# A small product turned round: router logits by expert instead of by token, and the way back to token order

## The reference, cut to what matters

```python
router_probs = jax.nn.softmax(jnp.einsum('bsh,he->bse', x, w_router), axis=-1)
gate_weights = jax.nn.softmax(jnp.einsum('bsh,he->bse', x, w_gating) / GATE_TEMP, axis=-1)
g = jnp.einsum('bsh,ehf->ebsf', x, w_gate)
u = jnp.einsum('bsh,ehf->ebsf', x, w_up)
h = jax.nn.silu(g) * u
expert_out = jnp.einsum('ebsf,efh->ebsh', h, w_down)
cw = router_probs * gate_weights
cw = cw / (jnp.sum(cw, axis=-1, keepdims=True) + 1e-09)
out = jnp.einsum('ebsh,bse->bsh', expert_out, cw)
```

## Time and profile before

| | |
|---|---|
| median of 3 runs | 1175.09 us (1173.66 to 1175.84) |
| the profiled execution | 1174.75 us |
| its span | 1172.9 us |
| granted TensorE clock over the span | 0.992 |
| TensorE busy | 1143.5 us (97%) |
| VectorE busy | 928.8 us (79%) |
| ScalarE busy | 677.4 us (58%) |
| GpSimd busy | 636.2 us (54%) |

### The profile page before, as it was taken

How to read it: one execution, slowest core, us unless ns; L and a number is a source line. 1 busy time by engine, 2 the same in 40 slices (tenths; PEclk the granted TensorE clock), 3 DMA queues, 4 the chain that set the end, 5 groups by cost and what they waited for, 6 DMA issues and landing times.

```text
span 1172.9 us, 16867 instructions
## 1 busy us (share of the span) xinstructions
PE 1143.5 (97%) x5190; PEld 943.3 (80%) x5190; DVE 928.8 (79%) x2032; ACT 677.4 (58%) x1293; POOL 636.2 (54%) x496
## 2 busy tenths in 40 slices
PE   5899999999999999999999999999999999999996
PEld 4678888888888888888888888888888888888885
DVE  8788787787878878787887878778787887878665
ACT  3366565656556566565656656565655656556553
POOL 4467464555546455564655546455554645556453
PEclk8999999999999999999999999999999999999999
DMA  4230110101111020110101111010111102011110
GB/s 122 64 111 25 46 45 34 40 20 46 46 43 49 1 72 19 45 46 37 41 15 57 35 46 46 32 42 19 46 46 41 50 1 72 19 46 37 37 46 10
DMA packets 43097, 49.75 MB, mean 42 GB/s; under 512 B 3424, under 2 KB 24576, under 8 KB 43008
## 3 DMA queue, kind: packets, MB, share of 16 engines
q1 hardware_dynamic: 43008, 48.67, 13.4%
HBM read 44.20 MB, written 4.46 MB: 41 GB/s over the span
## 4 chain that ended last, share of the span: by engine, by line
PE 95%; DVE 3%; issue 1%; POOL 0%; ACT 0%; DMA 0%; POOLq 0%; SPq 0%; ACTq 0%; DVEq 0%
PE g L240 10%; PE u L240 10%; PE u L242 10%; PE u L241 10%; PE g L242 10%; PE g L241 10%; PE y L242 10%; PE y L240 10%; PE y L241 10%; PE n_ps L247 2%; PE m_ps L240 1%; PE m_ps L242 1%; PE m_ps L241 1%; PE y L263 1%; PE m_ps L321 1%
## 5 line engine op out<-in xcount | busy, mean ns | idle before, releaser
L982 POOL TENSOR_TENSOR hid_lo<-hid,hid_hi 128x512 fp32r<-128x512 f32 x255 | 342.2, 1342 | 394.5 <-ACT hid_hi L483 394.3
L477 ACT ACTIVATE gate<-g 128x512 f32<-128x512 f32 x512 | 306.3, 598 | 363.0 <-PE g L242 360.5
L723 DVE TENSOR_TENSOR hid<-gate,u 128x512 f32<-128x512 f32 x512 | 349.2, 682 | 176.9 <-ACT gate L477 121.6
L483 ACT ACTIVATE hid_hi<-hid 128x512 fp32r<-128x512 f32 x512 | 320.6, 626 | 29.4 <-DVE hid L723 28.7
L240 PE MATMUL g<-xe_hi,w_hi 128*128 128x512 f32 x512 | 207.8, 406 | 0.0
L729 DVE TENSOR_TENSOR hid_lo<-hid,hid_hi 128x512 fp32r<-128x512 f32 x257 | 205.7, 800 | 0.4
L240 PE MATMUL u<-xe_hi,w_hi 128*128 128x512 f32 x512 | 200.0, 391 | 2.3 <-DVE hid L723 2.3
L240 PE MATMUL y<-hid_hi,w_hi 128*128 128x512 f32 x512 | 199.8, 390 | 0.2 <-ACT hid_hi L483 0.2
L242 PE MATMUL y<-hid_hi,w_lo 128*128 128x512 f32 x512 | 199.8, 390 | 0.0
L242 PE MATMUL g<-xe_hi,w_lo 128*128 128x512 f32 x512 | 199.6, 390 | 0.0
L241 PE MATMUL g<-xe_lo,w_hi 128*128 128x512 f32 x512 | 199.6, 390 | 0.0
(11 more groups left out here) (155 smaller groups left out, 1146.6 us busy)
## 6 DMA issues: line engine op xcount, KB each, us to landing
cw_b<-cw_scratch SPq DMA_DIRECT2D x128, 256.0 KB, 3.6
x_sb<-x_in SPq DMA_DIRECT2D x16, 256.0 KB, 4.0
x_out<-o_sb SPq DMA_DIRECT2D x16, 256.0 KB, 2.3
stage<-wgate_in SPq DMA_DIRECT2D x8, 256.0 KB, 2.7
stage<-wup_in SPq DMA_DIRECT2D x8, 256.0 KB, 3.0
stage<-wdown_in SPq DMA_DIRECT2D x8, 256.0 KB, 3.6
cw_scratch<-cw_t SPq DMA_DIRECT2D x16, 16.0 KB, 1.4
proj<-proj_in SPq DMA_DIRECT2D x1, 136.0 KB, 2.5
```

The source lines that it names most:

```text
L477: nc.scalar.activation(gate[:, k % 2, :], g_ps[k % 2][:], ACT.Silu).then_inc(gate_ready, 1)
L483: nc.scalar.activation(hid_hi[:, k % RING, :], hid[:, k % RING, :], ACT.Copy).then_inc(hi_ready, 1)
L723: nc.vector.tensor_tensor(hid[:, k % RING, :], gate[:, k % 2, :], u_ps[k % 2][:], ALU.mult).then_inc(hid_ready, 1)
L982: nc.gpsimd.tensor_tensor(hid_lo[:, k % RING, :], hid[:, k % RING, :], hid_hi[:, k % RING, :].bitcast(f32), ALU.subtract).then_inc(lo_pool, 1)
```

## The change

- **Products.** The router's high and low parts become the weights (128 x 32 columns) and all 512 tokens the moving operand: two products into 32 partitions of `m_ps`. `router` gets a third part of zeros (through 16 more columns of `proj_in`), so that the first product is low and high against `xe_hi` and the second high and zero against `xe_lo`.
- **The way back.** VectorE transposes 32 x 32 blocks from `m_ps` to `logits_t` (after unit 27; in chunk 0 after unit 0). SyncE then issues four transfers of 16 KB within SBUF, each of 32 partitions with four pieces of 128 bytes, to `raw`, with tokens on 128 partitions. The reduce of the softmax reads `raw`.
- **Places.** The softmax moves from k = 27 to 29 on VectorE, `silus` from 28 to 29 on ScalarE; in chunk 0 the softmax, `silus`, `exps`, `products` and `weights` move one unit back. In SyncE's stream the four transfers stand after the eighth spread and before the load of the next x.
- **Warming.** 24 products of three forms come before the first `bu` (`keep_warm_split`); `keep_warm_mixed` becomes `keep_warm(18)`, and VectorE's fill of its tile goes.

```diff
-SCALAR_AT = {..., "hi_xe": 26, "silus": 28}
+SCALAR_AT = {..., "hi_xe": 26, "silus": 29}
-VECTOR_AT = {..., "lo_xe": 26, "softmax": 27, "exps": 30, "products": 31}
+VECTOR_AT = {..., "lo_xe": 26, "logits_t": 27, "softmax": 29, "exps": 30, "products": 31}
...
+            def spread_logits(c):
+                sp.wait_ge(logits_turned, c + 1)
+                if c > 0:
+                    sp.wait_ge(raw_read, c)
+                blocks = logits_t[:].rearrange("c (j b q) -> c j b q", j=NT, q=SMALL)
+                for b in range(P // SMALL):
+                    sp.dma_start(raw[b * SMALL:(b + 1) * SMALL].rearrange("p j h q -> p j (h q)"),
+                                 blocks[:, :, b, :]).then_inc(raw_loaded, 16)
...
+                if first:
+                    spread_logits(0)
                 store_cw(c, par)
...
+                if not last:
+                    spread_logits(c + 1)
...
+            def keep_warm_split():
+                w, x = proj_hi[:, 0:P], act_hi[:]
+                for cols in (SMALL, NS):
+                    for i in range(8):
+                        nc.tensor.matmul(y_ps[1][0:cols, :], w[:, 0:cols], x, start=True, stop=True)
+                for i in range(8):
+                    nc.tensor.matmul(y_ps[1][:].rearrange("p (j t) -> p j t", j=NT), w,
+                                     act_hi[:].rearrange("p (j t) -> p j t", j=NT), start=True, stop=True)
...
-                    pe.wait_ge(raw_read, c)
+                    pe.wait_ge(logits_turned, c)
...
-                for j in range(NT):
-                    t, at = slice(j * P, (j + 1) * P), 4 * E * j
-                    nc.tensor.matmul(m_ps[:, at:at + 4 * E], xe_hi[:, par, t], router[:], start=True, stop=False)
-                    last = nc.tensor.matmul(m_ps[:, at:at + 2 * E], xe_lo[:, par, t], router[:, 0, :], start=False, stop=True)
-                last.then_inc(logits_ready, 1)
+                nc.tensor.matmul(m_ps[0:4 * E, :], router[:, 0:2, :], xe_hi[:, par, :], start=True, stop=False)
+                nc.tensor.matmul(m_ps[0:4 * E, :], router[:, 1:3, :], xe_lo[:, par, :], start=False,
+                                 stop=True).then_inc(logits_ready, 1)
...
             keep_warm(WARM[1])
+            pe.wait_ge(act_hi_ready, 1)
+            keep_warm_split()
             pe.wait_ge(proj_split, 2)
...
-            keep_warm_mixed()
+            keep_warm(WARM[3])
...
+            def mix_logits_t(c):
+                dve.wait_ge(logits_ready, c + 1)
+                nc.vector.transpose(logits_t[:], m_ps[0:SMALL, :]).then_inc(logits_turned, 1)
+
             def mix_softmax_in(c):
-                dve.wait_ge(logits_ready, c + 1)
+                dve.wait_ge(raw_loaded, RAW_LOADED * (c + 1))
...
                     if first and k == 0:
+                        mix_logits_t(0)
+                    if first and k == 1:
                         mix_softmax_in(0)
-                    if first and k == 1:
+                    if first and k == 2:
                         mix_exps(0)
                         mix_products(0)
-                    if k == (2 if first else VECTOR_AT["weights"]):
+                    if k == (3 if first else VECTOR_AT["weights"]):
                         mix_weights(c)
```

More of the change, by code:

```diff
@@ L46 @@
 SCALAR_AT = {"cw_t": 3, "hi_x": 8, "du": 8, "hi_w": 13, "fin_a": 14, "fin_b": 15, "z_a": 18, "z_b": 18,
-             "hi_xe": 26, "silus": 28}
+             "hi_xe": 26, "silus": 29}
 VECTOR_AT = {"weights": 1, "stats_x": 1, "var_x": 2, "norm_x": 3, "lo_x": 7, "enter": 8, "scan": 9,
              "fin_stats": 10, "fin_var": 10, "fin_shift": 11, "leave": 12, "lo_w": 13, "y": 15, "stats_y": 16, "var_y": 16,
-             "shift": 18, "stats_x1": 22, "var_x1": 22, "norm_x1": 24, "lo_xe": 26, "softmax": 27, "exps": 30,
+             "shift": 18, "stats_x1": 22, "var_x1": 22, "norm_x1": 24, "lo_xe": 26, "logits_t": 27, "softmax": 29, "exps": 30,
              "products": 31}
@@ L58 @@
 SMALL = 32
-PROJ = P + D + 2 * E
+PROJ = P + D + 4 * E
+RAW_LOADED = 16 * (P // SMALL)
 POOL_LO = (1, 3)
@@ L121, in build @@
         proj_hi, proj_lo = sb("proj_hi", [P, P + D], f32r), sb("proj_lo", [P, P + D], f32r)
-        router = sb("router", [P, 2, 2 * E], f32r)
+        router = sb("router", [P, 3, 2 * E], f32r)
+        logits_t, raw = sb("logits_t", [SMALL, SEQ]), sb("raw", [P, NT, 2, 2 * E])
         a_col, sines = sb("a_col", [NS // 2, 1]), sb("sines", [NS // 2, P])
@@ L146, in build @@
         w_hi_done, w_lo_done = sem("w_hi_done"), sem("w_lo_done")
-        const_ready, flat_ready = sem("const_ready"), sem("flat_ready")
+        const_ready = sem("const_ready")
         proj_split, omega_ready, trig_link, trig_ready = sem("proj_split"), sem("omega_ready"), sem("trig_link"), sem("trig_ready")
@@ L157, in build @@
         xe_turned, xe_hi_ready, xe_lo_ready = sem("xe_turned"), sem("xe_hi_ready"), sem("xe_lo_ready")
-        logits_ready, raw_read, lg_ready, silus_ready = sem("logits_ready"), sem("raw_read"), sem("lg_ready"), sem("silus_ready")
+        logits_ready, logits_turned, raw_loaded = sem("logits_ready"), sem("logits_turned"), sem("raw_loaded")
+        raw_read, lg_ready, silus_ready = sem("raw_read"), sem("lg_ready"), sem("silus_ready")
         cw_ready, cw_turned, cw_t_ready = sem("cw_ready"), sem("cw_turned"), sem("cw_t_ready")
@@ L488, in _ @@
             act.wait_ge(small_loaded, 32)
-            nc.scalar.activation(router[:, 0, :], proj[:, P + D:], ACT.Copy)
+            nc.scalar.activation(router[:, 1:3, :].rearrange("p h q -> p (h q)"), proj[:, P + D:], ACT.Copy)
             nc.scalar.activation(proj_hi[:], proj[:, 0:P + D], ACT.Copy).then_inc(proj_split, 1)
@@ L658, in mix_softmax_in @@
                 pair = "p j r -> p (j r)"
-                dve.wait_ge(logits_ready, c + 1)
+                dve.wait_ge(raw_loaded, RAW_LOADED * (c + 1))
                 nc.vector.tensor_reduce(out=lg[:].rearrange("p j r e -> p j (r e)"),
-                                        in_=m_ps[:, 0:NT * 4 * E].rearrange("p (j h q) -> p j q h", j=NT, h=2),
+                                        in_=raw[:].rearrange("p j h q -> p j q h"),
                                         op=ALU.add, axis=AX.X).then_inc(raw_read, 1)
@@ L756, in _ @@
             nc.vector.memset(cw_pad[:], 0.0).then_inc(const_ready, 1)
-            nc.vector.memset(hid[:, 0, :], 0.5).then_inc(flat_ready, 1)
-            dve.wait_ge(flat_ready, 1)
-            nc.vector.tensor_copy(hid_hi[:, 0, :], hid[:, 0, :]).then_inc(flat_ready, 1)
             slope = sum_sb
@@ L917, in body @@
                             mix_lo_xe(c + 1, 1 - par)
+                        if k == VECTOR_AT["logits_t"]:
+                            mix_logits_t(c + 1)
                         if k == VECTOR_AT["softmax"]:
@@ L1001, in _ @@
             pool.wait_ge(proj_split, 1)
-            nc.gpsimd.tensor_tensor(router[:, 1, :], proj[:, P + D:], router[:, 0, :].bitcast(f32), ALU.subtract)
+            nc.gpsimd.tensor_tensor(router[:, 0, :], proj[:, P + D:P + D + 2 * E], router[:, 1, :].bitcast(f32),
+                                    ALU.subtract)
             nc.gpsimd.tensor_tensor(proj_lo[:], proj[:, 0:P + D], proj_hi[:].bitcast(f32),
@@ L1064 @@
         "x_in": L0_attn_u,
-        "proj_in": np.concatenate([b_t, b_t, np.concatenate([c_t, c_t], axis=0), L0_ffn_w_router, L0_ffn_w_gating], axis=1),
+        "proj_in": np.concatenate([b_t, b_t, np.concatenate([c_t, c_t], axis=0), L0_ffn_w_router, L0_ffn_w_gating,
+                                   np.zeros((D, 2 * E), np.float32)], axis=1),
         "a_in": np.asarray(L0_attn_a_params).reshape(NS // 2, 1),
```

## The result

| | before | after |
|---|---|---|
| median, 4 runs each on one chip | 1174.39 us (1173.66 to 1175.84) | 1187.73 us (1186.47 to 1188.57) |
| profiled execution | 1174.75 us | 1188.57 us |
| its span | 1172.9 us | 1186.8 us |
| start-up, to the first unit's `g` | 44.91 us | 44.97 us |
| chunk 0 | 74.14 us | 79.18 us |

The ratio is 1.0111 [1.0098, 1.0125] (in brackets the 95% interval): slower by 1.1%, where I forecast 0.5% faster. Chunk 0 lost 5.0 us and the fourteen chunks behind it 8.5; the start-up and the tail stayed. The page of after: engines (busy us, share, instructions), the chain that ended last, and the new transfers (count, KB each, us to landing).

What follows compares the result with a forecast made beforehand. The prediction took TensorE, busy throughout chunks 1 to 14, as the bound. From 1174.75 us, -7.05 for the products and +1.3 for chunk 0 gave 1169.0; with 0.3 for the median, 1169.2 us, range 1166.8 to 1173.0.

Steps and rivals of the forecast that it cites:

- Products: TensorE, units 27 and 28: two long products replace eight small ones, saving 0.47 us a chunk, -7.05 us over 15 chunks.
- Transposition: VectorE, ahead of the transfers: 32 x 512 out of PSUM takes 0.69 us, off TensorE's path.
- Transfers: SyncE, chunks 1 to 15: four issues of 0.43 us, landing 1.4 us after issue, at no cost.
- the room of 1.2 us: Chunk 12, VectorE at k=29: the transferred data are there 1.2 us before the softmax needs them.
- the 4.0 us of the rival: Rival, each chunk: transfers land 4.0 us after the last issue, TensorE waits 0.9 to 1.15 us; 1185 to 1189, chance 0.08.
- ScalarE: silus at k=29 ahead of unit 30's gate and hid_hi of 29: fits with 0.25 us to spare, costing nothing.
- the k=0 to 2 that I had told the reader to look at: Sign of a wrong forecast: TensorE's u or y products waiting at k=0 to 2 after each softmax.
- ScalarE's blockade costs TensorE a few tenths: Rival, shared with new products not coming cheaper: 0.2 us a chunk over plan, +3 us, 1172; chance 0.06.
- Chunk 0: The uncovered round trip makes the normalised x ready at 60.9 to 61.9, delaying turn_x: +1.3 us (+0.6 to +1.9).
- the fall of the clock: Rival, chunk 0: TensorE's wait before turn_cw drops it to 1.2 GHz, +1.0 to +1.7 us, 1170.2 to 1170.9; chance 0.2.

Runs made afterwards that it cites:

- experiment 10: experiment 9 with GpSimd's first addition of a chunk at k=2 instead of 0, as in Experiment 5; 1168.67 us, 0.9952 of the kernel before.
- experiment 3: The kernel before with a VectorE transposition of the same shape added at k=27, which nothing reads; 1174.88 us, 0.9995 of the kernel before.
- experiment 1: The kernel before with only the two new places, softmax at k=29 and silus at 29; 1188.53 us, 1.0114 of the kernel before.
- experiment 2: The changed kernel with silus at k=30 instead of 29; 1174.31 us, 0.9998 of the kernel before.
- Experiment 5: The changed kernel, silus still at 29, with GpSimd's first addition of a chunk at k=2 instead of 0; 1177.09 us, 1.0016 of the kernel before.
- experiment 8: The changed kernel with seven warming products ahead of turn_cw at k=4 of chunk 0; 1185.81 us, 1.0094 of the kernel before.
- experiment 9: experiment 2 with chunk 0's logits made as before (eight products, no transfers, softmax at k=0); 1171.01 us, 0.9965 of the kernel before.

## Why the prediction was wrong

**Products: right.** I gave 4.66 us for units 27 and 28; 4.70 were measured, and experiment 10 keeps 0.446 a chunk of the 0.47 forecast.

**Transposition: right.** 0.697 us for a forecast 0.69, and experiment 3 shows it hidden.

**Transfers: too small a term, and a small loss by it.** The issue of one took 2.53/4 = 0.63 us, not the 0.43 of a plain load, and landing 1.8, not 1.4. So the room of 1.2 us was about 0.3. It held in most chunks: VectorE waited for `raw` four times, 3.2 us in all, 2.09 of them in chunk 0. The other three stand ahead of the three irregular chunks, which are 1.5 us longer together. The Trainium skill ("DMA: Bandwidth & Descriptors", Specifications) gives 512 B as the least size of a piece for full rate; the 128-byte pieces landed 0.4 us later than the 16 KB row of before, far from the 4.0 us of the rival. The sign is that of the page, but the row of before is a store to DRAM, so no run here shows what the size of the piece does by itself.

**ScalarE: the step that failed.** I saw that `silus` at k=29 stands ahead of the gate of unit 30 and of `hid_high` of 29, and worked out when `hid_low` of 29 is ready for its down product: "It fits, with 0.25 us to spare." It did fit: no `y` product waits. But I followed that one product only, and concluded that "in each chunk the long way costs nothing". The gate of unit 30, which the same block holds back, has another reader, VectorE. I did not follow it further:

1. ScalarE idles 2.12 us, and the gate of unit 30 is 1.5 us late (experiments 1 and 2).
2. VectorE idles meanwhile for 0.95 us and then has the same work in less time.
3. Of GpSimd's four operations that start between 2.0 us before the next chunk and 6.2 us after its start, two keep their places (2.19 us after the start, against 2.07 in experiment 2, and 6.15 in both) and two come 1.5 us later. VectorE's, 1.0 to 2.5 us later, fall on them: four that took 0.31, 0.15, 0.91 and 0.15 us in experiment 2 take 0.75, 1.08, 1.41 and 1.25, which is 3.0 more. (By the groups, against the kernel before, it is (31.5 + 21.6)/16 = 3.3 us a chunk.)
4. `hidden` of unit 2 of the next chunk starts 2.5 us later in its chunk than in experiment 2 (624.65 - 615.72 = 8.93 against 6.38), past the two buffers' slack, and `u` of unit 4 waits.

Experiment 5 shows link 3 to be needed: with GpSimd's addition moved, four fifths of the wait (3.02 to 2.27) go while ScalarE stays blocked; the last fifth comes with two collisions that stayed. The wait came at k=4, behind the k=0 to 2 that I had told the reader to look at. Among the rivals this was "ScalarE's blockade costs TensorE a few tenths", 0.2 us a chunk, in a rival with a chance of 0.06. The mechanism had a name and a price a fifth of the true one (0.95), because I took it as a delay of one item and not as a backlog that meets another engine. The only rival that gave 1185 to 1189 did so by late transfers, which were not the cause: experiment 1 has none and loses as much.

**Chunk 0: right in kind, a quarter in size.** I gave +1.3; it lost 5.0. The normalised x was ready at 61.5, as worked out (60.9 to 61.9). What I had wrong is that it is not what TensorE waited for: `weights` was not done near 58.4 but at 60.55, since its last steps met GpSimd (1.22 and 1.03 us for 0.15 and 0.22) and the landing was late by another 1.4. So `turn_cw` stood 3.63 us, 4.4 later than before (56.24), with a whole unit between it and `turn_x`. With it came the fall of the clock, a rival with a chance of 0.2: 2.7 us in the profiled execution of after and 1.5 in that of experiment 2, by the units of experiment 8, where I gave 1.0 to 1.7. In after it fell before the wait that I had named, in experiment 2 behind it.

**The sum.** From the profiled executions: products -15 x 0.45 = -6.8; wait of unit 4, 14 x 0.95 = +13.3; three irregular chunks +1.5; chunk 0 +5.0, and +0.45 for the saving of its k=27, which the first term holds already; start-up and tail +0.2. That is +13.7, for a measured 13.8. Without the ScalarE term the forecast would have been 1169.2 + 3.7 (chunk 0) and some for irregular chunks, near 1174: what experiment 2 measured.

**What stays open.** The rows show that VectorE's operation ends when GpSimd's does, in the forms named; they don't show which resource it is. The irregular chunks of after and of experiments 2 and 9 all stand behind a chunk in which VectorE waited for `raw`. A 16 KB fetch of instructions beside the issues was there in all but one of these cases (0.19 us, experiment 9), but that it delays them was not tried by itself. In experiments 2 and 9 a wait of 0.20 and one of 0.19 us made the next chunk 0.8 us longer; in experiment 10 a wait of 0.29 us, with a fetch beside it too, cost nothing. So with GpSimd's addition moved a delay of this size is covered; one near 0.57 us did not occur there. A version of the change whose transfers are issued with fewer, larger pieces was not tried.

## What to carry to other kernels

When a step that waits is moved, follow every item queued behind it, on every engine that reads it, until idle time has swallowed the delay; one product that "fits" is not the answer. An engine at 80% has its gaps in places, and a shift by 1 us can put its operations on those of a neighbour that did not shift. Put the consumer of a late value one place behind its producer, not beside it: one number, `silus` at 30 instead of 29, was worth 13.4 us here (1187.73 to 1174.31), twice what the change itself could bring.

## What the runs showed of the hardware

- A VectorE operation of 150 ns lasted up to 1.25 us while GpSimd ran a 128 x 512 operation, and ended within 0.02 us of it. It hit `den` (128 x 4) and `hid_low`; `hidden`, with one input in PSUM, stayed at 681 ns (682 before), and the reduces, with one input, at 188 and 206 (186 and 212). The Trainium skill ("GPSIMD Engine Reference", its table's row on SBUF interfaces) says that GpSimd contends with VectorE instructions that have two SBUF inputs; these rows agree. I had not expected it to hold an operation for as long as the other one lasts, whatever its size.
- A transposition of 32 x 512 in 32 x 32 blocks from PSUM took 697 ns, as long as any other 512-column operation from PSUM (692).
- A transfer of 32 partitions with four pieces of 128 bytes took 0.63 us to issue on SyncE and 0.76 on ScalarE (1.52/2); a plain load took 0.43.
- In after the granted clock stood at 0.50 for 10.2 us. It fell at 56.2, 1.2 us after a wait of 1.89 us, and stayed down through the wait of 3.63 us and 5.8 us of work behind it. In experiment 2, with waits of 1.90 and 3.96 us in the same places, it did so from 61.3 to 64.8 only, once work had begun again. In experiment 8, with seven warming products in the gap, it did not fall in chunk 0 after 50 us.
